# A gated-recurrence and mixture-of-experts kernel: x copies by halves, the rows' high halves one chunk later, a gate chunk between transpose and spread

## The reference

```python
# layer 1: a gated recurrence, 4 heads of 64
xp = x @ W_in.T;  gates = xp @ W_gate.T + b_gate
i, f, o, c~ = exp, sigmoid, sigmoid, tanh of the four parts
c  = f * c + i * c~                                   # scan over the sequence
h  = o * tanh(c * rsqrt(mean(c*c) + EPS) * rms_w)     # mean over one head
y  = h @ W_out.T
# layer 2: 16 experts, top 4 by router logits
logits = x @ router_weight.T + router_bias
out = sum over the chosen experts of score * (((up + 1) * glu) @ down + bias)
```

## Time and profile before

| | |
|---|---|
| median of 3 runs | 796.6 us (795.14 to 798.18) |
| the profiled execution | 802.32 us, its span 800.5 us |
| PE busy | 635.2 us (79% of the span) |
| DVE / ACT / POOL busy | 537.2 / 458.7 / 396.1 us |
| mean granted TensorE clock | 0.859 of full speed |

### The profile page before, as it was taken

The page is one execution under the profiler, slowest core; times in us unless marked ns, Lnnn a source line. Parts: engine busy times, 40 slices in busy tenths (PEclk is TensorE's granted clock), DMA queues, the critical chain, the costliest instruction groups (busy, mean ns, idle before and its releaser), DMA issues.

```text
span 800.5 us, 13282 instructions
## 1 busy us (share of the span) xinstructions
PE 635.2 (79%) x3658; PEld 408.9 (51%) x3658; DVE 537.2 (67%) x1570; ACT 458.7 (57%) x933; POOL 396.1 (49%) x300
## 2 busy tenths in 40 slices
PE   5887979598998752302999999999999999997450
PEld 2344636264565541201666666666666666664230
DVE  3637487778878978500777777777777777771892
ACT  2777686547546533101666767767767767762242
POOL 0012214654845737752466666666666656565121
PEclk9979798889989856555999999999999999997555
DMA  7966754799522223253677777776777676645987
GB/s 250 423 238 106 150 92 71 224 318 347 158 86 101 89 72 119 106 207 99 112 114 110 111 113 111 108 114 109 113 113 114 108 114 102 108 58 76 350 149 102
DMA packets 111895, 115.35 MB, mean 144 GB/s; under 512 B 31730, under 2 KB 101506, under 8 KB 110162
## 3 DMA queue, kind: packets, MB, share of 16 engines
q0 software_dynamic: 35456, 50.35, 37.2%
q1 hardware_dynamic: 76370, 64.16, 26.7%
HBM read 55.15 MB, written 59.31 MB: 143 GB/s over the span
## 4 chain that ended last, share of the span: by engine, by line
PE 59%; DVE 12%; DMA 8%; POOL 7%; ACT 6%; issue 5%; SPq 2%; POOLq 0%; ACTq 0%; DVEq 0%
PE PS L633 8%; PE PS L634 8%; PE PS L635 8%; PE PS L502 7%; POOL routed L916 6%; PE PS L624 4%; PE PS L653 4%; PE PS L641 4%; PE PS L654 4%; PE PS L655 4%; PE PS L525 2%; PE PS L533 2%; DMA W<-w_dn 2%; DMA W<-neg_mem 1%; DVE small L1325 1%
## 5 line engine op out<-in xcount | busy, mean ns | idle before, releaser
L942 POOL DMA_INDIRECT sums<-arena x144 | 223.2, 1550 | 143.8 <-ACT arena L702 71.5
L916 POOL DMA_INDIRECT routed<-arena,small x128 | 142.7, 1115 | 90.6 <-DVE small L1162 45.3
L1303 DVE TENSOR_SCALAR arena<-PS,small 128x256 f32<-128x256 f32 x144 | 78.3, 544 | 126.7 <-ACT arena L875 124.7
L702 ACT ACTIVATE arena<-PS 128x512 f16<-128x512 f16 (+1 forms) x180 | 105.1, 589 | 78.7 <-PE PS L624 45.7
L502 PE MATMUL PS<-arena 128*128 128x512 f32 x256 | 134.0, 668 | 10.7 <-ACT arena L702 10.6
L875 ACT ACTIVATE arena<-PS,small 128x256 f32<-128x256 f32 x144 | 68.1, 473 | 104.1 <-PE PS L635 104.1
L633 PE MATMUL PS<-W,arena 128*128 x288 | 110.2, 382 | 0.0
L634 PE MATMUL PS<-W,arena 128*128 x288 | 110.1, 382 | 0.0
L635 PE MATMUL PS<-W,arena 128*128 x288 | 109.9, 382 | 0.0
L502 PEld LDWEIGHTS PS<-arena 128*128 128x128 f32 x256 | 51.9, 214 | 69.3 <-issue 65.8
L624 PE MATMUL PS<-ident,arena 128*128 128x128 f16 x576 | 56.3, 221 | 36.7 <-DMA arena<-routed 35.9
(11 more groups left out here) (164 smaller groups left out, 1023.3 us busy)
## 6 DMA issues: line engine op xcount, KB each, us to landing
arena<-routed SPq DMA_DIRECT2D x144, 128.0 KB
W<-w_gu SPq DMA_DIRECT2D x8, 1024.0 KB, 23.6
W<-neg_mem POOLq DMA_DIRECT2D x16, 512.0 KB, 8.5
sums<-zero SPq DMA_DIRECT2D x2, 4096.0 KB, 26.2
W<-sums SPq DMA_DIRECT2D x16, 512.0 KB, 8.8
X<-x SPq DMA_DIRECT2D x8, 512.0 KB, 4.8
W<-w_dn SPq DMA_DIRECT2D x4, 1024.0 KB, 11.4
out<-X SPq DMA_DIRECT2D x8, 512.0 KB, 3.0
```

The costliest lines, as they stand in the source:

```text
L702: return nc.scalar.activation(o, i, ACT.Copy, **kw)
L916: pool.indirect_dma_start(routed, bass.IndirectOffsetOnAxis(ap=idx, axis=0), rows[b][:, jk // TOPK, :], None).then_inc(rows_sent[lane], 16)
L942: pool.indirect_dma_start(sums[j % SUMS], bass.IndirectOffsetOnAxis(ap=dst[j % MU], axis=0), yb[u], None, compute_op=ALU.add).then_inc(y_s ...
L1303: L.send(v.tensor_scalar(up[j % 2], acc[:, FF:2 * FF], gu_hi, gu_lo, ALU.min, ALU.max))
```

## The change

Three edits in the block stage:

1. The last chunk's product k = 0 raises a semaphore of its own, `gate_half`. The x copy k = 0 waits for that, the copy k = 1 for the chunk's end; before, both waited for the end.
2. `row_high` of a block moves on ACT from behind chunk 7 and `norm_y` of one step to behind chunk 0 of the next step, so `square` and chunk 0 now stand ahead of it. The last block's stays where it was.
3. On PE, `rms_spread` and `transposes_x2` move from ahead of chunk 4 to behind it. `rms_transpose` stays ahead. So chunk 4 now stands between transpose and spread, and `logits` follows directly on `transposes_x2`.

```diff
                     last = mm(PS[:, 2 + c % 2, :], WcT[:, k, c * P:(c + 1) * P], xT[:, k, :],
                               start=(k == 0), stop=(k == KT - 1))
+                    if c == CHUNKS - 1 and k == 0:
+                        last.then_inc(gate_half, 1)
...
-                    if c == 3 and mid:
+                    if c == 4 and mid:
                         rms_spread(s - 1)
-                    if c == 3 and old:
+                    if c == 4 and old:
                         transposes_x2(s - 2)
-                    if c == 4 and old:
                         logits(s - 2)
...
             def evac_x(t):
                 for k in range(KT):
                     act.wait_ge(xT_mm, 2 * t + (k + 1))
+                    if t and k == 0:
+                        act.wait_ge(gate_half, t)
+                    if t and k == KT - 1:
+                        act.wait_ge(gate_mm, 8 * t)
                     copy(xT[:, k, :], PS[:, k, :]).then_inc(xT_ready, 1)
...
                     if c == CHUNKS - 1 and on(s, -1):
-                        act.wait_ge(gate_mm, 8 * s + 8)
                         evac_x(s + 1)
...
-                    if c == CHUNKS - 1 and old:
+                    if c == CHUNKS - 1 and s == NBLK + 1:
                         row_high(s - 2)
+                    if c == 0 and on(s, 3):
+                        row_high(s - 3)
```

More of the change, by code:

```diff
@@ L296, in build @@
         gate_mm, gate_act, f_ready = sem("gate_mm"), sem("gate_act"), sem("f_ready")
+        gate_half = sem("gate_half")
         u_ready = sem("u_ready")
```

## The result

| | before | changed |
|---|---|---|
| median, same session | 797.4 us (795.1 to 800.5) | 818.1 us (814.0 to 821.0) |
| profiled execution / its span | 802.3 / 800.5 us | 821.0 / 819.2 us |
| mean granted clock | 0.859 | 0.834 |
| start of the scatter of block 5 | 295.41 us | 315.97 us |

The ratio is 1.025, 95% interval 1.019 to 1.032. The forecast had the direction and the place, but the loss is nearly three times as large, 20.7 instead of 7.5 us, and outside the range.

What follows compares the result with a forecast made beforehand. The chain of waits up to the scatter of block 5 was taken to bound the kernel; the steps' terms, 2.4 - 1.9 + 2.2 + 2.3 + 0.3 + 2.2 = +7.5 us, gave 804.0 us, range 791 to 811.

Steps and rivals of the forecast that it cites:

- What bounds the kernel: Chain of waits read back from the tile stage: only what moves the start of block 5's scatter (295.41 us) counts.
- Edits 1 and 2: ACT ahead of mean_square: it starts 1.45 us earlier, 10.2 behind out_product; DVE limits the gain to 0.5 to 1.4 a step.
- Edit 3's order: PE from rms_transpose to out_product's end: 12.2 us at full clock, against 11.58 in step 5 and 11.24 in step 7.
- The gap: PE between transposes_x2 and logits: idle from 5.05 to 6.7 us behind rms_transpose, until slot_ready.
- The fall: PE's clock drops in most steps after 1.65 us idle and 1.96 of narrow logits, hitting out_product and the chunks behind.
- rival (d): Two clock falls a step, one over spread and x2 transposes, one over out_product; some 815 us; chance 0.06.
- a fall costs 2.2: Mean price in us of one PE clock drop in the kernel before, ends 1.3 and 3.3; makes 12.2 into 14.4.
- Rival (c): Dearer clock falls: down over logits and all of out_product, 3.3 us each, and also at rms_transpose; 810 us; chance 0.12.
- Steps 3 and 4: Chunk 4 done earlier, so squares release DMAs and the x load sooner, -1.4 us; step 4's window 16.1 against 13.89, +2.2.
- The sum: Gains and losses of steps 1 to 7 up to the scatter of block 5: together +7.5 us.
- The rule of the Trainium skill: TensorE transposes do not count as activity for the clock gate; by it two falls a step were likely.

Runs made afterwards that it cites:

- filler: Changed kernel plus four unused 256-column products on PE between x2 transposes and logits; 805.6 us, ratio 1.007 to before (first, in a session with ScalarE stalls: 811.1, 0.992).
- chunk 5 runs: Changed kernel with chunk 5 moved from behind out_product to between x2 transposes and logits; 804.7 us, ratio 0.986, then 801.2 us, ratio 1.002, to before.
- narrow filler run: Changed kernel plus seven unused 2-column products between x2 transposes and logits; 824.7 us, ratio 1.033 to before.
- edit 3 with the filler: Kernel before with only chunk 4 ahead of the spread, plus four unused 256-column products between x2 transposes and logits; 799.7 us, ratio 1.003 to before.
- filler ahead of T: Edits 1 and 2 without edit 3, plus four unused 256-column products on PE ahead of rms_transpose; 799.8 us, ratio 1.000 to before.

## Why the prediction was wrong

**What bounds the kernel** held: the sum must be made up to the scatter of block 5, and the change there is 20.6. That this is so near the 20.7 of the medians is partly luck, since the two profiled executions are 18.7 apart.

**Edits 1 and 2** were right as steps. `mean_square` starts 10.3 behind `out_product`'s end (230.05 - 219.76), predicted 10.2. From there to T the gains were predicted as 0.5, 1.4 and 1.0 for steps 5, 6 and 7. Counted from `out_product`'s end of the step before to T they are 0.4, 2.6 and 1.0: step 6 took 20.34 before (T at 224.16, `out_product` ends at 203.82) and 17.72 now. The surplus in step 6 is a milder fall: from `mean_square` to the end of the two chunks PE took 8.68 before and 7.2 now (230.05 to 237.2), so that T now waits for DVE (0.24). The 0.5 of step 3 did not come: 20.25 against 20.32. That the gains show nothing in the time when the two edits run without the third was not foreseen.

**Edit 3's order** was right: 12.2 from T to `out_product`'s end at full clock. The filler and chunk 5 runs, which have this order and something wide in the gap, show 11.9 where no fall comes, 12.05 with the 0.16 that these rows leave out. The gap was predicted from 5.05 to 6.7 behind T, and measured with `slot_ready` last, logits at 6.5.

**The fall** was predicted in the right stretch, and falls are most of the loss: the filler, which takes part of them away, gives back 15.6 of 21.8 us. What is left, 0.3 and 0.7%, is the order together with the falls that remain. Its cause was half right. The prediction had 1.65 of idle and 1.96 of logits bring the clock down; in the changed kernel it was down 0.3 us into the gap, behind spread and x2 transposes, and the idle and the logits came after. That the spread and the transposes do not hold the clock was the premise of rival (d), at 0.06; it had two falls a step, where step 6 has one long one. In step 6 of the narrow filler run the clock came down with almost no idle there (0.10 in the whole window).

**The failed step is the term "a fall costs 2.2", so 14.4 for T to `out_product`.** Step 2 met it (14.32). In step 6 the measured window is 16.37, 4.2 above 12.2: 1.6 on the logits (3.60 against 1.96) and 2.7 on `out_product` (6.22 against 3.55). Steps 5 and 3 lost more, since chunk 4 ran at the low clock as well (17.95 and 19.72 for the window). I had averaged the falls of the kernel before, in which chunks stood directly behind or two short pieces on, and several of them spoilt only two chunks. In the new stretch idle and narrow work are still ahead when the clock falls: 1.55 us of idle and 3.60 of logits, and it comes back only near the end of `out_product`. That the narrow work keeps it down is my reading of this; no run changes only what follows a fall. Rival (c) had the form of this, with the clock down over the logits, all of `out_product` and at T too, with 3.3 each, too small too, and I gave it 0.12.

**Steps 3 and 4** went the other way. I took -1.4 from T to the `squares` behind chunk 4 (+0.3 if the clock is down at T). PE waits 4.11 us ahead of T now (3.17 before), the clock falls in this wait (1.00 in 117.80:119.70, 0.50 in 119.90:121.80), and the chain of step 3 reads:

```profile
122.19 3.41 PE PS L503 x4
125.61 3.71 PE PS L528 x16
...
133.46 1.05 ACT W L798 x2
```

`squares` start 11.65 behind T instead of 9.23, +2.4. T of step 3 itself was 2.8 late (121.81 against 118.99), most of it from step 1, where the sum had +2.4 and -0.5. Through the DMAs of the earlier trace rows both move T of step 4: 163.62 against 158.03, +5.6 where the sum had +0.5.

**The sum again, with what was measured**, each against before: T of step 4 +5.6; step 4's window 18.31 - 13.89 = +4.4; step 5 -0.4 and 17.95 - 11.58 = +6.4; step 6 -2.6 and 16.37 - 12.74 = +3.6; step 7 -1.0 and 16.39 - 11.24 = +5.2; step 8 -0.6. Together 20.6. The sum had +2.2, +2.3, +0.3 and +2.2 for steps 4 to 7.

**The rule of the Trainium skill** on transposes (TensorE: Matmul & The Clock Gate, Part 4) can't be judged by these runs. In step 6 of the filler run the clock held at 1.00 over chunk, spread, transposes and filler, where the transposes are the only full-width work in 2.9 us (232.16 to 235.06). In the changed kernel it fell just behind the spread and the same transposes. None of the runs separates the two.

## What to carry to other kernels

Where TensorE's work is a chain of short pieces, look at how wide the work is that stands together: a block of wide products that "only covers a wait" may be what keeps the clock, and moving it away can cost more than the wait that it removes elsewhere. Price a fall by what lies on the chain behind it, not by the mean of other falls; here, where idle and narrow products came first, the clock stayed down through them and into the wide work. A test is cheap: put unused wide products, and as a control narrow ones, into the gap and see whether more work makes the kernel faster.

## What the runs showed of the hardware

- TensorE's clock fell with PE busy 15.15 of 15.25 us, where two-column and 16-column products stood behind the x2 transposes. With products of 256 columns for about the same time (1.89 against 1.62) in the same place there was no fall in steps 6 and 7 (11.90 and 11.89 us at 1.00), and none in steps 3 and 5 to 7 of edit 3 with the filler.
- The clock also fell directly behind the spread (16-row products) and the x2 transposes, with about 0.2 us of idle (changed kernel, step 6), and behind the spread with 0.6 us of idle (filler ahead of T, step 6). It does not do so each time: in step 5 of the kernel before it stayed at 1.00 over the same pieces.
- In one session, in all four profiled kernels, ScalarE stood still for some microseconds where no engine of the program is named as what held it. From the timeline of the first run with chunk 5 in the gap:

```profile
208.19 1.14 ACT L812 ACTIVATE W<-W,small 128x1024 f16<-128x1024 f32 x1
213.41 0.60 ACT L706 ACTIVATE arena<-PS 128x512 f32<-128x512 f32 x1 [4.08 <-remote]
```

The profile puts it down to another core or an unknown queue. Its cause was not found. The kernel before had a median of 821 us in that session and of 797 to 803 us in the others; it was not profiled there, so that the same stalls slowed it is likely but not shown. The ratios of that session were not all repeated: chunk 5 in the gap had 0.986 there and 1.002 in a quiet one.
